# Mu's norms spread over the partitions: by a row in memory and a broadcast load, or by matmuls on an identity

## The reference

```
x = x + xattn(layernorm(x), ctx, pos, Wq, Wkv, Wout, bout)      # 32 heads of 8, rotary q and k
x = x + ffn(layernorm(x), gamma, beta, mu, scale, W1, b1, W2, b2)

ffn:  x_n  = l2norm(x_ln, -1) * scale
      mu_n = mu / max(sqrt(sum(mu * mu, axis=0)), 1e-12)        # mu: (256, 16 experts, 128 slots)
      logits = x_n . mu_n ;  dispatch, combine = two softmaxes of logits
      slot_in -> gelu(W1) -> W2 -> out by combine
```

## Time and profile before

| | |
|---|---|
| median of three runs | 475.66 us |
| the profiled execution | 477.61 us |
| its span, first to last instruction | 475.7 us |
| mean granted TensorE clock | 0.985 of full speed |
| busy: TensorE, its weight loads | 93%, 80% |
| busy: VectorE, ScalarE, GpSimd | 82%, 60%, 38% |
| L1160, 32 records (half of them the second pass of a float32 matmul) | 106.3 to 137.7 us |
| L580, 4 copies | 586 ns each |

### The profile page before, as it was taken

One profiled execution on the slowest core, in us unless ns is written; L12 is line 12 of the kernel. 1 busy time (PEld: TensorE's weight loads), 2 busy tenths in 40 slices (PEclk: granted clock), 3 DMA queues, 4 the chain that ended last, 5 costly groups with the idle time before them and its releaser, 6 DMA issues.

```text
span 475.7 us, 12795 instructions
## 1 busy us (share of the span) xinstructions
PE 444.3 (93%) x4816; PEld 382.1 (80%) x4816; DVE 389.0 (82%) x857; ACT 286.7 (60%) x553; POOL 182.8 (38%) x322
## 2 busy tenths in 40 slices
PE   0679999999999999999999999999999999999996
PEld 0557787878887778878888988988988988988985
DVE  6689888898889877977977977977977877887775
ACT  3457777778888666365466466457457447447443
POOL 4479998379996332114112112112112112202100
PEclk9979999999999799999999999999999999999999
DMA  8930000000003000223213223312312312312330
GB/s 231 271 152 23 3 3 23 1 4 1 3 1 72 3 2 1 52 56 83 68 52 84 68 55 77 77 50 72 83 50 66 88 50 61 99 44 55 99 92 22
DMA packets 27815, 28.54 MB, mean 60 GB/s; under 512 B 10960, under 2 KB 19072, under 8 KB 27520
## 3 DMA queue, kind: packets, MB, share of 16 engines
q1 hardware_dynamic: 27392, 27.48, 22.1%
q10 hardware_dynamic: 384, 0.52, 0.5%
HBM read 9.11 MB, written 2.10 MB: 24 GB/s over the span
## 4 chain that ended last, share of the span: by engine, by line
PE 74%; DVE 14%; POOL 4%; SPq 3%; DMA 2%; issue 2%; ACT 1%; ACTq 0%; DVEq 0%; POOLq 0%
PE bank L1025 13%; PE bank L1027 12%; PE bank L1026 12%; PE bank L1241 10%; PE bank L1121 6%; PE bank L1263 6%; PE bank L1104 3%; PE bank L1085 3%; PE bank L1142 2%; SPq L293 2%; DVE kT L758 2%; DMA xa<-in_x 2%; DVE pT L904 2%; DVE on L777 1%; DVE pb L932 1%
## 5 line engine op out<-in xcount | busy, mean ns | idle before, releaser
L904 DVE STREAM_TRANSPOSE pT<-eb 128x512 f32<-128x512 f32 x64 | 44.5, 700 | 38.3 <-ACT eb L618 35.0
L1241 PE MATMUL bank<-w_raw,eb 128*128 128x130 f32 x512 | 60.8, 276 | 1.3 <-DVE w_raw L895 1.3
L1241 PEld LDWEIGHTS bank<-w_raw,eb 128*128 128x128 f32 x512 | 58.5, 190 | 2.7 <-DVE w_raw L895 2.3
L629 ACT ACTIVATE pb<-pb 128x768 f32<-128x768 f32 (+1 forms) x48 | 37.2, 774 | 28.2 <-DVE pb L932 28.2
L1025 PE MATMUL bank<-mun_h,xlT_l 128*128 128x512 f32 x128 | 52.1, 407 | 0.0
L932 DVE TENSOR_TENSOR pb<-bank,rh 128x384 f32<-128x384 f32 x96 | 49.3, 513 | 3.3
L624 ACT CAST xlT_h<-bank 128x256 fp32r<-128x256 f32 x16 | 5.9, 372 | 76.1 <-PE bank L1213 76.1
L618 ACT ACTIVATE eb<-bank,nshift,rn 128x512 f32<-128x512 f32 x64 | 46.2, 776 | 7.8 <-PE bank L1027 7.6
L1027 PE MATMUL bank<-mun_h,xlT_h 128*128 128x512 f32 x128 | 50.5, 395 | 0.0
L545 ACT COPY pT<-bank 128x512 f32<-128x512 f32 x64 | 37.6, 588 | 21.3 <-PE bank L1104 20.5
L1026 PE MATMUL bank<-mun_l,xlT_h 128*128 128x512 f32 x128 | 50.5, 394 | 0.0
(11 more groups left out here) (159 smaller groups left out, 1155.4 us busy)
## 6 DMA issues: line engine op xcount, KB each, us to landing
mu_raw<-pT SPq DMA_DIRECT2D x248, 64.0 KB, 2.0
mu_raw<-in_L_ffn_mu SPq DMA_DIRECT2D x1, 2048.0 KB, 10.1
out<-w_raw SPq DMA_DIRECT2D x16, 128.0 KB, 1.9
xa<-in_x SPq DMA_DIRECT2D x1, 1536.0 KB, 8.5
w_raw<-in_L_ffn_W SPq DMA_DIRECT2D x2, 512.0 KB, 10.1
w_raw<-in_L_ffn_W SPq DMA_DIRECT2D x1, 1024.0 KB, 7.3
xa<-in_x SPq DMA_DIRECT2D x1, 512.0 KB, 3.5
ctile<-in_ctx SPq DMA_DIRECT2D x1, 512.0 KB, 5.2
```

Of the source, the lines that this page charges most:

```text
L904: v.transpose(eblk[:, :, 4 * c:4 * c + 4, :].rearrange("p m e j -> p e m j"), eb[:, 4 * c:4 * c + 4, :].rearrange("p e (m j) -> p e m j", ...
L1241: m = mm(bank[HB[i]][:, n * 2 * HC:(n + 1) * 2 * HC], eb[:, e, :], xw[:, e, :], start=True, stop=True)
```

## The change

The four `spread_norms` on TensorE and the four `rb_copy` on ScalarE go, and with them TensorE's wait for the copy. SP gets two transfers and two waits, between its last load of ctx and the loads that wait for mu: when mu_r is ready it writes the 2048 factors to a row in device memory, in the order of mu's columns, waits for that, and loads the row into all 128 partitions of mu_rb. `scale_mu` waits once, before its first bank, for that load.

```diff
+        norm_row = nc.dram_tensor("norm_row", (ES,), F32, kind="Internal").ap()
...
+            sp.wait_ge(mur_ready, 1)
+            sp.dma_start(norm_row.rearrange("(e s) -> s e", s=SLOTS), mu_r[:, 1, :], allow_slow_non_contiguous=True)                .then_inc(row_loaded, 16)
+            sp.wait_ge(row_loaded, 16)
+            sp.dma_start(mu_rb, row(norm_row, ES)).then_inc(rb_loaded, 16)
+
             sp.wait_ge(mu_ready, NQ * KD)
...
             def scale_mu(c, k):
-                if k == 0:
-                    pool.wait_ge(rb_ready, c + 1)
+                if c == 0 and k == 0:
+                    pool.wait_ge(rb_loaded, 16)
...
-            def rb_copy(c):
-                act.wait_ge(rb_filled, c + 1)
-                a.copy(mu_rb[:, c * BANK:(c + 1) * BANK], bank[6][:]).then_inc(rb_ready, 1)
...
-                if norms is not None:
-                    rb_copy(norms)
...
-            def spread_norms(c):
-
-                pe.wait_ge(mur_ready, 1)
-                pe.wait_ge(pT_ready, (8 + c) * 4 - 1)
-                for e in range(4):
-                    m = mm(bank[6][:, e * SLOTS:(e + 1) * SLOTS],
-                           mu_r[:, 1, 4 * c + e].unsqueeze(1).broadcast_to([P, P]), ident[:], start=True, stop=True)
-                m.then_inc(rb_filled, 1)
...
-                if 8 <= s < 8 + NQ:
-                    spread_norms(s - 8)
...
-                if 8 <= s < 8 + NQ:
-                    pe.wait_ge(rb_ready, s - 7)
```

More of the change, by code:

```diff
@@ L148, in build @@
         mur_ready = sem("mur_ready")
-        rb_filled = sem("rb_filled")
-        rb_ready = sem("rb_ready")
+        row_loaded = sem("row_loaded")
+        rb_loaded = sem("rb_loaded")
         muscale_step = sem("muscale_step")
@@ L576, in xT_high, with step @@
                 a.copy(flat(xT[0][:, t % 2]), bank[7][:, 0:3 * P]).then_inc(xT_split, 1)
-            def rb_copy(c):
-                act.wait_ge(rb_filled, c + 1)
-                a.copy(mu_rb[:, c * BANK:(c + 1) * BANK], bank[6][:]).then_inc(rb_ready, 1)
-            def step(s, norms=None):
+            def step(s):
                 if s >= 1:
                     pT_copy(s - 1, 3)
-                if norms is not None:
-                    rb_copy(norms)
                 exp_group(s, 0)
@@ L663, in _ @@
             for s in range(TILES):
-                step(s, s - 8 if 8 <= s < 8 + NQ else None)
+                step(s)
             act.wait_ge(shift_ready, 1)
```

## The result

The changed kernel is slower. In the first comparison four runs took 482.93 to 488.88 us, median 484.2, against 475.61 us for the kernel before: ratio 1.0199, 95% interval 1.0128 to 1.027. In a later one five runs took 482.99 to 489.42 us, median 487.84, against 476.38, ratio 1.0205 (1.0156 to 1.0255). A ratio is always the time over that of the kernel before, with its 95% interval. The profiled execution took 482.93 us, the fastest of its four runs, with a span of 481.0 us; mean clock 0.975.

The account below looks back on a forecast made before the run. TensorE was taken to set the pace, with GpSimd nearly full in steps 8 to 11. Net +1.95 us from GpSimd's delay and +0.45 for the clock made +2.4: 478.1 us, slower by 0.5%, 8-in-10 range 475.4 to 485.

Parts of the forecast that it names:

- the first transfer's price: SP's store of the 2048 factors to device memory: 4.0 us from issue to landing, ends 1.9 and 10.1.
- D: Delay of GpSimd's first scale_mu, from 109.38 to 112.83 because both transfers must land: 3.45 us.
- 1.95 and 0.45 for the clock: Net loss at step 12's transposes: 1.95 us from GpSimd's lateness, 0.45 more from a clock drop in step 9.
- The load: SP's 1 MB broadcast load of the norms after the store: 4.6 us, ends 3.2 and 7.3.
- GpSimd's turn: GpSimd's repeating work in steps 8 to 11: stays at 10.18 us while TensorE's step falls to 9.49.
- The half clock: TensorE's 2.45 us wait in step 9 was expected to bring a clock drop costing 2.5 us, mostly hidden.
- the waits of about 0.7 us in steps 10 to 12: TensorE waiting for GpSimd's rope_sums, which never catch up: about 0.7 us in each step.
- The 2.76 us of matmuls: TensorE time saved by dropping sixteen matmul pairs in steps 8 to 11: 4 x 0.69 us.
- Slow small stores: Rival: 4-byte writes to memory cost much more, store 10.1 us, D 9.55, time 484.2 us; chance 0.20.
- Clock drops again and again: Rival: waits in steps 10 to 12 bring another clock drop, another 2.5 us, 480.6 us; chance 0.13.
- The old drop moves away: Rival: the known clock drop in step 13 does not come, 2.5 us come back, 475.6 us; chance 0.11.
- The transfers fit into the slack: Rival: both transfers within 6.6 us before scale_mu, D under 1.5 us, gain 1.5 us, 474.1 us; chance 0.09.

Follow-up runs that it names:

- experiments 3: Changed kernel with the same 2048 pieces of 4 bytes written to SBUF, not device memory; ratio 1.0020 to the kernel before.
- experiment 4: Changed kernel with the 2048 pieces of 4 bytes written to device memory 512 bytes apart; ratio 1.0044 to the kernel before.
- experiments 1 to 11: Eleven follow-up kernels, each an edit of the changed kernel or of the kernel before; ratios to the kernel before from 0.997 to 1.0129.
- 5: Changed kernel with the four pairs of scale_mu in steps 9 to 12 in place of 8 to 11; ratio 1.0129 to the kernel before.
- 8: Kernel before plus a store of all 2048 factors, each 512 bytes from the next, for which nothing waits; ratio 1.0010.
- 10: Changed kernel with scale_mu in steps 9 to 12 and the row transposed, then stored in pieces of 512 bytes; ratio 1.0031 to the kernel before.
- 9: Kernel before with scale_mu in steps 9 to 12 in place of 8 to 11, everything else as it was; ratio 1.0044.
- experiment 2: Changed kernel without the store; the broadcast load brings the first row of mu instead; ratio 0.997 to the kernel before.
- 6: Kernel before plus the store of the 2048 neighbouring factors, for which nothing waits; ratio 1.0098.
- 7: Kernel before plus a store of half the factors, 1024 neighbouring pieces of 4 bytes, for which nothing waits; ratio 1.0129.

## Why the prediction was wrong

The step that failed is the first transfer's price: "I take 4.0 us". It measured 10.45 and 10.46 us, beyond even the far end of 10.1. D follows from it, 9.50 us instead of 3.45, and the change of steps 8 to 12, 7.45 us instead of 1.95 and 0.45 for the clock.

Most of the rest held. The load took 4.23 us (4.6 predicted). GpSimd's turn was 10.06 us, not the 10.18 of the kernel before, which is worth 0.36 us over three turns. GpSimd had idle time only before scale_mu and none before rope_sums of steps 10 to 13. L1064, now L1065, waited for GpSimd. GpSimd did not catch up until step 12. The half clock came with the wait in step 9 and lengthened that step by 1.8 us, all but 0.1 of it covered: TensorE reached step 12's transposes at 156.38 where GpSimd had finished at 156.30. So the waits of about 0.7 us in steps 10 to 12, which the prediction gave before it took the clock into account, did not come. The 2.76 us of matmuls did come back, as four steps of 9.49. With stores that land in 4.02 and 4.15 us, experiments 3 and 4, the kernel is 1.0 and 2.1 us slower, and the forecast said 2.4: the mechanism was right, and of its terms the store was mis-sized. Outside it stands the idle time in step 8, on which more below.

Why that term? The value was taken between the store of 1 KB pieces with the pieces' moving time added, 3.1 us, and posb's load, 5.4; the end of 10.1 was a load under full traffic. None of these rows has small pieces written next to each other in device memory: posb's are loaded into SBUF, where the 16 of a partition do lie in a row. And the earlier trace rows told how fast small pieces are read and moved, which was right even here. The transfers of the kernel after from 103.1 to 106.5 us and from 106.5 to 113.6:

```profile
DMA packets 2064, 0.01 MB, mean 2 GB/s; under 512 B 2064, under 2 KB 2064, under 8 KB 2064
```

```profile
DMA packets 0, 0.00 MB, mean 0 GB/s; under 512 B 0, under 2 KB 0, under 8 KB 0
```

All pieces have moved by 106.5 (in finer windows by 105.5), about as soon as forecast; for 7 us more nothing moves and the store has not landed. In experiment 4 the last of as many pieces moves at about 107.9, and the store lands at 109.09, 1.2 us later. The cost is in the completion, which no row of the kernel before shows.

*Slow small stores* was the rival that came true, with 484.2 us as its time, and it had a chance of 0.20. That it names the median of the first comparison to the tenth is luck: its 10.1 us was taken from loads under full traffic, and the second comparison gave 487.84. Its reason was only half right. The Trainium skill ("DMA: Bandwidth & Descriptors", Specifications) speaks of a read-modify-write below 512 bytes; here 128 pieces of 64 bytes landed in 1.42 us and 2048 lone pieces of 4 bytes in 4.15, so being below that size is not enough for 10 us. By the runs it takes pieces of 4 bytes next to each other; whether a read-modify-write is at work no run shows.

*Clock drops again and again* did not happen: steps 10 to 12 took 9.49 us each, because TensorE, and no longer GpSimd, came last there. *The old drop moves away* came in part: in step 13 the half clock lasted 3.4 us where it was 6.8, and step 13 was 1.50 us shorter. Whether the change did that is not shown. Of the profiles of experiments 1 to 11 seven have the short form, three the long one (5, 8 and 10), and experiment 4 has none there; 8 and 9 differ in it though both keep the kernel before's steps 8 to 12. *The transfers fit into the slack* needed D under 1.5 us; experiment 2, at 1.21, is in line with it, by 0.3%.

What none of the cases had is the standing still in step 8. In the changed kernel it is hidden, as rope_sums, done at 126.08, would have held TensorE anyway; experiments 5, 6 and 7 bare it, with a step 8 that is 4.8, 4.0 and 5.1 us longer, idle time and half clock together.

**What stays open.** What the engines lack in that stretch. TensorE's instructions come in handfuls with no semaphore between them, ScalarE stands though its operand is ready, both go on within 0.1 us of each other in the changed kernel (111.79 and 111.83), and GpSimd runs through. Late delivery of instructions, for which the profiles have transfer queues of their own, would look like this; but it was only argued, and no run tested it. The traces don't settle it: in the changed kernel no transfer of those queues moves between 103.1 and 117 us, so TensorE went on at 111.79 without a new one having moved, while one that moved before could still have landed late. Nor is it known from which size or distance on neighbouring pieces land quickly. Last, the comparisons give 8.6 us (medians) and 9.8 us (1.0205) for the changed kernel, some 1 to 2 us more than its steps 8 to 12 account for.

## What to carry to other kernels

Price a store by where its pieces land as well as by how many there are: 2048 single elements of 4 bytes written next to each other into device memory took 10.5 us to land here, as many 512 bytes apart 4, and one small transpose that makes the rows whole brings the store to 1.4. When work on an engine in order is made to wait, ask what stands behind it in that engine's queue, and compare its turn (10.06 us) with that of the engine it feeds (9.49): it says at once whether a delay is ever made up. And before long GpSimd work is moved, look at which short VectorE operations it will then run beside.

## What was not expected of the hardware

- After a store of neighbouring 4-byte pieces to device memory TensorE and ScalarE stand still or stutter, from some 7 us after its issue (6.8 to 7.2 in five profiles): for 1.9 us in the changed kernel, and in kernels that don't wait for the store for 2.7 us (2048 pieces) and 3.8 us (1024), with a step 8 of 14.2 and 15.2 us in place of 10.2. With 2048 pieces 512 bytes apart step 8 takes 10.2 us.
- The pieces of such a store have moved after 3 us and it lands after 10.45.
- A VectorE instruction on 11 columns takes 0.17 us alone and up to 1.26 us (tensor_tensor) or 1.24 us (tensor_scalar, experiment 5; 1.14 in experiment 9) beside a GpSimd instruction on 512 columns, ending within 0.05 us of it.
- GpSimd's multiplication on 512 columns took 1.54 us where one input had a stride of 64 bytes, and 1.28 where it had none.
